# A macaron block on one core: mean and spread of 1/deviation of the feed-forward stages as products of a high and a low part

## The reference

```python
def _layernorm(x, axis=-1, eps=1e-05):
    m = jnp.mean(x, axis=axis, keepdims=True)
    v = jnp.var(x, axis=axis, keepdims=True)
    return (x - m) / jnp.sqrt(v + eps)
...
        x_prev = jnp.concatenate([jnp.zeros((B, 1, C), x.dtype), x[:, :-1, :]], axis=1)
        xr = mu_r * x + (1.0 - mu_r) * x_prev
        xk = mu_k * x + (1.0 - mu_k) * x_prev
        r = jax.nn.sigmoid(jnp.einsum('btc,dc->btd', xr, W_r))
        k = jnp.einsum('btc,dc->btd', xk, W_k)
        k_act = jnp.square(jax.nn.relu(k))
        out = r * jnp.einsum('btc,dc->btd', k_act, W_v)
...
    x = x + 0.5 * _L0_ffn_ref(_layernorm(x, axis=-1), ...)
    x = x + _L0_attn_ref(_layernorm(x, axis=-1), ...)
    x = x + 0.5 * _L0_ffn_ref(_layernorm(x, axis=-1), ...)
```

## Time and profile before

| | |
|---|---|
| median of 3 runs | 3533.43 us (3529.58 to 3539.18) |
| profiled execution | 3535.1 us, of which the span of its instructions 3533.3 us |
| mean granted clock of PE | 0.972 |
| PE busy | 3299.1 us, 93% of the span |
| DVE busy | 2739.6 us, 78% |
| POOL busy | 1845.0 us, 52% |
| ACT busy | 1582.4 us, 45% |

### The profile page before, as it was taken

One profiled execution on the slowest core, in us unless ns is written; L12 is line 12 of the kernel. 1 busy time (PEld: TensorE's weight loads), 2 busy tenths in 40 slices (PEclk: granted clock), 3 DMA queues, 4 the chain that ended last, 5 costly groups with the idle time before them and its releaser, 6 DMA issues. The chain is left out here.

```text
span 3533.3 us, 191423 instructions
## 1 busy us (share of the span) xinstructions
PE 3299.1 (93%) x83236; PEld 2757.8 (78%) x83236; DVE 2739.6 (78%) x4491; ACT 1582.4 (45%) x2344; POOL 1845.0 (52%) x1707
## 2 busy tenths in 40 slices
PE   7999998799999999995999999999996997999999
PEld 5888886576766767674999999999995775888887
DVE  6767665787888878784899999999997866676765
ACT  4555553577777777773112121111213433545454
POOL 1232322465555665654787887888785431323232
PEclk8999999899999999997999999999997998999999
DMA  3122222232322323225677777777774772212121
GB/s 119 71 95 83 88 90 91 78 100 78 102 79 84 101 74 99 86 76 133 182 200 202 198 200 199 197 197 200 197 200 136 238 226 107 107 71 107 71 107 60
DMA packets 486526, 452.84 MB, mean 128 GB/s; under 512 B 55489, under 2 KB 448833, under 8 KB 467265
## 3 DMA queue, kind: packets, MB, share of 16 engines
q1 hardware_dynamic: 484160, 449.56, 42.1%
q10 hardware_dynamic: 2304, 2.49, 0.3%
HBM read 331.33 MB, written 120.60 MB: 128 GB/s over the span
## 5 line engine op out<-in xcount | busy, mean ns | idle before, releaser
L350 POOL TENSOR_TENSOR ffn_out<-ffn_gate,ffn_xres 128x512 f32<-128x512 f32 x128 | 223.5, 1777 | 779.8 <-DVE ffn_gate L254 779.4
L784 DVE SCALAR_TENSOR_TENSOR ain_conv<-ain_padded,ain_taps,ain_conv 128x512 f32<-128x512 f32 x384 | 416.8, 1085 | 13.8 <-DVE ain_tail L781 0.3
L1464 ACT ACTIVATE rec_u<-rec_ps_end 128x256 f32<-128x256 f32 x128 | 49.2, 384 | 645.7 <-PE rec_ps_end L1516 645.7
L885 POOL TENSOR_TENSOR ain_conv<-ain_conv,ain_term 128x512 f32<-128x512 f32 x192 | 272.4, 1419 | 16.0
L1232 POOL TENSOR_TENSOR rec_d_norm<-rec_dmat,rec_early 128x512 f32<-128x512 f32 x128 | 162.9, 1273 | 181.6 <-DVE rec_dmat L1314 181.6
L940 ACT ACTIVATE ain_buf<-ain_conv 128x512 f32<-128x512 f32 x192 | 121.0, 630 | 233.5 <-POOL ain_conv L885 147.6
L46 PE MATMUL ffn_ring<-ffn_mixkh,ffn_wkh 128*128 128x512 f32 x512 | 218.7, 427 | 6.5 <-DVE ffn_mixkl L196 6.5
L46 PE MATMUL ffn_ring<-ffn_mixrh,ffn_wrh 128*128 128x512 f32 x512 | 216.0, 422 | 9.2 <-DVE ffn_mixrl L306 9.2
L46 PE MATMUL ffn_ring<-ffn_mixkh,ffn_wkl 128*128 128x512 f32 x512 | 203.8, 398 | 0.0
L46 PE MATMUL ffn_ring<-ffn_mixrh,ffn_wrl 128*128 128x512 f32 x512 | 202.6, 396 | 0.0
L46 PE MATMUL ffn_ring<-ffn_mixkl,ffn_wkh 128*128 128x512 f32 x512 | 201.7, 394 | 0.0
(11 more groups left out here) (249 smaller groups left out, 10351.9 us busy)
## 6 DMA issues: line engine op xcount, KB each, us to landing
rec_early<-coeffs SPq DMA_DIRECT2D x512, 128.0 KB, 3.0
streams<-ain_buf SPq DMA_DIRECT2D x48, 1024.0 KB, 5.1
rec_qkv<-streams SPq DMA_DIRECT2D x126, 384.0 KB, 3.3
rec_qk_pe<-streams SPq DMA_DIRECT2D x127, 256.0 KB, 3.3
rec_late<-coeffs SPq DMA_DIRECT2D x504, 64.0 KB, 2.2
ffn_xres<-in_x SPq DMA_DIRECT2D x16, 1024.0 KB
ain_x<-x SPq DMA_DIRECT2D x16, 1024.0 KB, 4.9
gate<-ain_gate SPq DMA_DIRECT2D x16, 1024.0 KB, 6.7
```

Of the source, the lines that this page charges most:

```text
L350: added = nc.gpsimd.tensor_tensor(out[:, m, :], gate[:, m, :], xres[:, m, :], ALU.add)
L784: nc.vector.scalar_tensor_tensor(out=out[:], in0=pad[:, n:n + TOK], scalar=taps[:, u // KT, u % KT, n:n + 1], in1=out[:], op0=ALU.mult, op ...
L885: nc.gpsimd.tensor_tensor(out[:], out[:], term[:], ALU.add).then_inc(pool_conv, 1)
L1464: nc.scalar.activation(u[:], ps_end[:, :, 1, :], ACT.Copy).then_inc(u_ready, 1)
```

## The change

In both feed-forward phases the mean and the spread become two `F32R` products each, of the high and the low part of their data with a constant. `sum1` gets a high part `sum_h` (a copy on ACT, `sum_round`, between its copies of mix r and mix k) and a low part `sum_l` (a subtraction on DVE, `sum_rest`, behind the mixes of k). The mean of a tile waits for `sum_l`. The mean of tile 0, which is made of two halves, and that of tile 1 stay as they were. `rstd_tok` is split into a high and a low part by two small instructions on DVE, and `rstd_diag` holds the diagonals of both, 1024 columns instead of 512. The constants 1/512 and 1 are held in the reduced type too. The variance stays as it was.

```diff
-        rstd_diag = sb("rstd_diag", [P, KT, P])
+        rstd_diag = sb("rstd_diag", [P, 2, KT, P], F32R)
+        rstd_split = sb("rstd_split", [P, 2, KT], F32R)
+        sum_h, sum_l = sb("sum_h", [P, TOK], F32R), sb("sum_l", [P, TOK], F32R)
+        mean_r, ones_r = sb("mean_r", [P, P], F32R), sb("ones_r", [P, P], F32R)
...
+            dve.wait_ge(consts, 1)
+            nc.vector.tensor_copy(mean_r[:], mean_w[:])
+            nc.vector.tensor_copy(ones_r[:], ones[:])
...
+            def sum_rest(t):
+                dve.wait_ge(sum_high, t - 1)
+                nc.vector.tensor_tensor(sum_l[:], sum1[:], sum_h[:].bitcast(F32), ALU.subtract).then_inc(sum_split, 1)
...
                 nc.vector.reciprocal(rstd_tok[:], std_tok[:]).then_inc(inverted, 1)
                 dve.wait_ge(inverted, t + 1)
-                nc.vector.tensor_tensor(rstd_diag[:], ident[:].unsqueeze(1).to_broadcast([P, KT, P]),
-                                        rstd_tok[:].unsqueeze(2).to_broadcast([P, KT, P]), ALU.mult).then_inc(diagonal, 1)
+                nc.vector.tensor_copy(rstd_split[:, 0, :], rstd_tok[:]).then_inc(rstd_high, 1)
+                dve.wait_ge(rstd_high, t + 1)
+                nc.vector.tensor_tensor(rstd_split[:, 1, :], rstd_tok[:], rstd_split[:, 0, :].bitcast(F32),
+                                        ALU.subtract).then_inc(rstd_low, 1)
+                dve.wait_ge(rstd_low, t + 1)
+                nc.vector.tensor_tensor(rstd_diag[:], ident[:].unsqueeze(1).unsqueeze(1).to_broadcast([P, 2, KT, P]),
+                                        rstd_split[:].bitcast(F32).unsqueeze(3).to_broadcast([P, 2, KT, P]),
+                                        ALU.mult).then_inc(diagonal, 1)
...
                     sums(t + 2)
                 if ahead:
                     mixes(t + 1, "k", 1)
+                if ahead == 2:
+                    sum_rest(t + 2)
...
+            def sum_round(t):
+                act.wait_ge(summed, t)
+                act.wait_ge(mean_done, t)
+                nc.scalar.activation(sum_h[:], sum1[:], ACT.Copy).then_inc(sum_high, 1)
...
                     high(t + 1, "r", 0)
+                if more == 2:
+                    sum_round(t + 2)
                 if more:
                     high(t + 1, "k", 1)
...
             def mean(t):
-                pe.wait_ge(summed, t)
-                nc.tensor.matmul(ps_mean[:], mean_w[:], sum1[:], start=True, stop=True).then_inc(mean_done, 1)
+                if isinstance(t, int) and t == 1:
+                    pe.wait_ge(summed, 1)
+                    nc.tensor.matmul(ps_mean[:], mean_w[:], sum1[:], start=True, stop=True).then_inc(mean_done, 1)
+                else:
+                    pe.wait_ge(sum_split, t - 1)
+                    nc.tensor.matmul(ps_mean[:], mean_r[:], sum_h[:], start=True, stop=False)
+                    nc.tensor.matmul(ps_mean[:], mean_r[:], sum_l[:], start=False, stop=True).then_inc(mean_done, 1)
...
             def spread_rstd(t):
                 pe.wait_ge(diagonal, t + 1)
-                nc.tensor.matmul(ps_rstd[:], ones[:], rstd_diag[:].rearrange("p j n -> p (j n)"), start=True,
-                                 stop=True).then_inc(spread, 1)
+                for part in range(2):
+                    last = nc.tensor.matmul(ps_rstd[:], ones_r[:], rstd_diag[:, part].rearrange("p j n -> p (j n)"),
+                                            start=(part == 0), stop=(part == 1))
+                last.then_inc(spread, 1)
```

More of the change, by code:

```diff
@@ L108, in ffn_phase @@
         v_used, out_ready = sem("v_used"), sem("out_ready")
+        sum_high, sum_split, rstd_high, rstd_low = sem("sum_high"), sem("sum_split"), sem("rstd_high"), sem("rstd_low")
         x0_loaded, r_loaded = [sem(f"x0_loaded{k}") for k in range(2)], sem("r_loaded")
@@ L438, in _ @@
             high(0, "k", 1)
-            with act.Fori(0, NT - 1) as t:
-                slot(t, True)
-            slot(NT - 1, False)
+            with act.Fori(0, NT - 2) as t:
+                slot(t, 2)
+            slot(NT - 2, 1)
+            slot(NT - 1, 0)
         @block.tensor
```

## The result

The changed kernel takes 3567.68 us (median of 6, 3562.14 to 3571.28) beside 3533.17 us for the kernel before in the same sessions: a ratio of 1.0093, interval 1.0082 to 1.0104. It is slower by 34.5 us; by the interval it could be between 29 and 37. The profiled execution has a span of 3560.4 us at a mean granted clock of 0.974, 27.1 us above that of before.

The account below looks back on a forecast made before the run. PE, busy 200.00 of 200 us in the feed-forward loop, was taken to bound the kernel. Longer slots (+32.8 us) plus phase starts and ends (+1.1) gave +33.9 us: median 3567 us, range 3556 to 3580.

Parts of the forecast that it names:

- The wait: In 28 feed-forward slots PE's mean waits about 1.9 us for sum_l; each slot grows 1.17 us, +32.8 us in all.
- S: Start of the spread on PE in a slot, the point from which the forecast measures both engines' times.
- DVE's order is the cause: sum_l, 0.69 us, stands on DVE behind the four mixes of k, 2.73 us, so the mean starts 1.57 us later.
- The matmul savings: Mean and spread drop from 0.86 us to two products of 0.229 us, 0.46 together: 0.40 us saved each.
- ScalarE's copy costs nothing: The sum_h copy, 0.63 us, fits ScalarE's 6.87 us idle gap ahead of its copy of mix k.
- The diagonals fit: The spread's diagonals, seen by PE at 124.85, are ready 0.11 us before its weight load, so nothing is added.
- Rival C: The diagonals are late too in the loop, up to +10 us: 3577; 12 in 100.
- The starts: At each feed-forward phase's start, small steps and wider diagonals lie on the path: +0.95 us per phase.
- Rival D: The clock falls in the new idle time: 2.7 us a slot, 77 us over 28 slots, 3644; 4 in 100.
- A: The mean doesn't wait and all matmul saving is kept: -22 us, 3511; 5 in 100.
- B: Part of the mean's wait is hidden and the result is within 0.3%; 5 in 100.

Follow-up runs that it names:

- sums_early: The full change with DVE's channel sums ahead of mix r's low part and sum_l ahead of the mixes of k: 3514.70 us, 0.9934 of the kernel before.
- rest_after_first_mix: The full change with only the sum_l subtraction moved, behind the first of the four mixes of k: ratio 0.9941 to the kernel before.
- the runs behind the gates: The full change with the sum_l subtraction moved behind gate 1, 2, 3 or 4 on DVE: 1.0162, 1.0358, 1.0339, 1.0498 of the kernel before.
- spread_only: The full change without its mean half, so new spread and old full-precision mean: ratio 0.9971 to the kernel before.
- mean_high_only: The full change without sum_l, the mean of tiles 2 to 15 being one product of sum_h: ratio 0.9918 to the kernel before.
- diag_later: The full change with an unused 128x512 product on DVE ahead of the diagonals: ratio 1.0106 to the kernel before.

## Why the prediction was right

Forecast 3567, +33.9 us; measured 3567.68, +34.5 us. That the two agree to 0.6 us is luck in part: the interval of the difference is 29 to 37 us, and the one profiled execution of each kernel has 27.1. What was shown is the mechanism and the 1.2 us a slot.

- *The wait.* Predicted: the mean at S + 18.78 + 0.05 and 0.10 for the missing early weight load; measured S + 18.82. The idle time of DVE ahead of `ffn_xn` fell by 1.32 us, predicted 1.3. In the waits it is 1.7 us, not 1.9, 47.7 us in all and not 50 to 55. This is only how the record counts: the last product before the stop is recorded 0.39 us long where the pace is 0.229, so 0.16 us of the stop lie under it; with them it is 52 us in all. The slot has the true size: 36.80 us, predicted 36.8.
- *That DVE's order is the cause.* Shown by `sums_early`, `rest_after_first_mix` and the runs behind the gates: the same instructions in other places give 0.9934 to 1.0498, the upper end with a lower clock and a longer subtraction in it.
- *The matmul savings.* Predicted 0.40 us for each. `spread_only` shows 0.39 a slot and `sums_early` 0.81 for both. So the 0.86 us of the earlier trace rows was the right price of a full-precision pair; with 0.92 us it would have been 0.46 us for each.
- *ScalarE's copy costs nothing.* Shown by `mean_high_only`.
- *The diagonals fit.* Right, and with more room than the 0.11 us that I counted: in `diag_later` weight load and product both start 0.05 us after the diagonals, so that a late weight load does not delay its product by its whole length. Rival C was less likely than I put it, and would have cost less than its 10 us.
- *The starts.* DVE's first normalisation starts at 21.15 instead of 20.17, 0.98 us later, predicted 0.95. But the profiled `ffn1` gave it back at once: `ffn_xn` of the next tile starts at 54.10 where it was at 55.08 before. PE's windows of before and of after in this place show that it was the clock:

```profile
50.00:52.00 2.00, 2.00 (x7) 0.56 0.00 0
52.00:54.00 2.00, 2.00 (x7) 0.59 0.00 0
```

```profile
50.00:52.00 2.00, 2.00 (x13) 1.00 0.03 8
52.00:54.00 2.00, 2.00 (x10) 1.00 0.00 0
```

The kernel before ran these products largely at the lower of the two clocks in its profiled execution, the changed one at the full one. In `ffn2` it was the same: from the first work of DVE to this row 53.96 us before and 52.30 after, and in the two windows of 2 us ahead of the row the clock was 0.50 and 0.71 before and 1.00 in both after. This is part of why the profiled spans differ by 27.1 us only. By DVE's first work on data in `ain` it is 15.2 us (613.95 against 629.16), in `ffn2` 14.8 (607.6 against 622.4), and the untouched phases between were 2.9 us shorter in this execution. Whether the clock at the start falls this way each time, one trace of each can't tell.
- *Rival D.* The clock holds at stops of 1.7 us, as the earlier trace rows had it. Those rows say only that 1.7 us of 5 were idle, but it was one stop:

```profile
1119.05 1.13 PE L1023 MATMUL ain_ps_rows<-ain_sq,ain_head_sum 128*128 128x512 f32 x2 [1.70 <-ACT ain_sq L949]
```

  The price that I named for D, 2.7 us a slot, is near what the dearest slots paid: 2.4 us at 3.6 us of stop, 2.9 at 4.8. Others paid less, down to nothing at 3.6 and 1.3 at 4.8. The rule of the Trainium skill (TensorE: Matmul & The Clock Gate, HAM oscillation), that waits between bursts can throttle the clock anew each time, is not contradicted. The waits of that section's example last some 3 to 5 us, longer than the forecast's 1.9, so the prediction went too far in putting the loop near D by it. The trace agrees where the stop is 4.8 us; at 3.6 us it does in 20 of 26 slots behind gate 2, and at 2.3 us, shorter than in that example, still in four of 26.
- *A and B* did not come true. The condition that I named for A, a `sum_l` 1.8 us earlier on DVE, is more than met in `sums_early`, where it is ready 1.8 us before PE wants it, and its time is near what A had: -24 us measured, -22 worked out.

`sums_early` beats both kernels: 3514.70 us, 0.9934 of before.

## What to carry to other kernels

When an input of the bounding engine gets one more step on another engine, look up where in that engine's queue the step lands. Here 0.69 us of work cost 1.9 us of wait because 2.73 us of other work stood ahead of it, and moving it ahead of that work, together with the sums that it needs, turned a loss of 0.9% into a gain of 0.7%. Where the helping engine has an idle place, put the step there. And keep the stops of PE short: here those of 1.7 us cost only themselves, those of 2.3 us also cost clock in a few slots, and those of 4.8 us in all.

## What was not expected

- A stop of 2.3 us already cost clock in four of 26 slots, 1.4 us each; at 3.6 us the same stop cost nothing, 1.6 or 2.4 us on top from slot to slot; at 4.8 us every slot paid, 1.3 to 2.9 us.
- The same subtraction of 128x512 took 0.68 us behind the mixes and behind gate 1, 1.38 behind gate 2, 0.79 behind gate 3 and 1.42 behind gate 4, each time in all 28 slots. Behind every gate it ran in part or wholly beside GpSimd's additions (in the change it did not), behind gate 1 without getting longer. What sets its length was not tried.
